# A transformer block on one core: token features spilled in their own layout, one engine's loop written out, one pair of steps on ScalarE swapped

## The chip, the cores and the metric

The kernel runs on one core of a Trainium2 chip. The metric is device time in microseconds (us) of one launch. The engines are named as in the profile: PE is TensorE's matmuls (PEld its weight loads), DVE VectorE, ACT ScalarE, POOL GpSimd, SP SyncE, which here issues all DMAs, in program order, on one queue.

## The reference, cut to what matters

```python
x = x + layernorm(attn(layernorm(x), Wq, Wk, Wv, Wo))          # x: (4, 1024, 512) float32
h = layernorm(x)
gate = h @ spline(gate_cp).T                                   # (4096 tokens, 2048)
up   = h @ spline(up_cp).T
x = x + layernorm((silu(gate) * up) @ spline(down_cp).T)
```

`attn` is attention over the 512 channels (a softmax of 512 x 512 scores for each of the four batches). `spline` fills a dense weight of 2048 x 512 from some 8,000 control points by cubic interpolation, so each run of 128 neighbouring weights is a few cubic pieces.

## The kernel before, in words

An attention block (to about 391 us of the span) and then an FFN block. The FFN never builds the dense gate and up weights. Each token's layernormed row is multiplied by a table of polynomial and window functions, which gives "token features" z: for each of 4 channel tiles (k) 16 unit tiles (t) of 8 powers (f) and 8 window functions. gate and up are then products of z with small coefficient matrices (`s_all`), one pair for each of 16 hidden tiles.

**Groups and steps.** The 4096 tokens are 8 groups (g) of 512, and each group has 16 steps (i), one for each hidden tile; four steps are a quad (j). A step on each engine:

- PE: `gate_up` two steps ahead (gate into `gbank` once `silu_done` says that it was read, up into `ubank` once `inter_done` says so), in every second step `moment_pair`, then `part`, one of 16 pieces of the down projection of the group before (12 matmuls into `ybank`, some pieces three more). In two steps of a quad also `turn` and `products`, which make the features of a tile of tokens six tiles ahead.
- ACT: `high` (cast of inter to f16 `act`, line 1372) of one step and `silu_at` (gated from `gbank`, line 1376) of the step behind it; in between by quad `feats.high` (h_hi), two `z_high` (z_hi, line 1034), `y_out`, `o_norm`, `moment_hi`.
- DVE: `product` (inter, line 1445), and by quad `turn_copy` (hT), `z_low` (z_lo, line 1065), `norm` (xn, line 1049), `low` (h_lo), two statistics, `o_finish` (x_res, line 1476, which adds the residual), in two quads of a group's end also `moment_lo` (line 1451).
- POOL: `low` (act, line 1331) and small scales.

**Turning the features.** The products leave z with (t f) on partitions and (k, tokens) along the row. gate and up want (k f) on partitions and (t, tokens) along the row. So each group is spilled to a DRAM tensor (`token_features`) and loaded again. Before the change the spill does the turn: `spill` (line 1005) issues 12 DMAs of 64 KB for each half of the partitions, each to rows of 1 KB in the order (k, f, t), and `load_z` (lines 1145 and 1147) reads a half in two DMAs, whose rows are 8 KB in one piece. `regroup` in the FFN's SP program does this for the next group after quad 1, when the four tiles are made; PE wants half 0 of it two steps ahead of the group's end (step 14), half 1 eight steps later.

**SP's order around it.** In quad 1 SP does `finish` of tile 0 (the store of x_res, line 1268), then `regroup`, and only then `reload` (the residual of tile 2 into the freed buffer, line 1264), which DVE's `o_finish` wants in step 14. In the other quads `reload` follows `finish` directly, after the store has landed.

**Loops.** All five engines run groups 0, 1, 6 and 7 as straight code and groups 2 to 5 as a loop of two passes (`schedule`), so PE branches back at the end of group 3.

Of the kernel before, what the change touches and what calls it, by code (L numbers as in the profile page):

```python
# [63 lines left out]
def attention_block(nc, x, wq, wk, wvT, wo, x1, raw_ctrl, unit_ctrl, unit_coef, job_in, s_dram, d_dram,  # L64
# [20 lines left out]
    with ExitStack() as ctx:  # L85
# [116 lines left out]
        last_banks = [chain[:, 3, :], chain[:, 2, :]]  # L202
        SPILLS = feats.SPILLS
        assert XR == 4 and NT == 2 * K
# [4 lines left out]
        def _(sp):  # L209
# [40 lines left out]
            def body(b, more):  # L250
# [41 lines left out]
                for t in range(NT):  # L292
                    if not more and t == NT - 1:
                        sp.wait_ge(job_ready, (b + 2) * JOBS)
                        sp.dma_start(d_dram[b], job_out[:]).then_inc(d_stored, 16)
                    sp.wait_ge(x1_ready, b * NT + t + 1)
                    sp.dma_start(x1_t[b * NT + t], x_res[:, t % XR, :]).then_inc(x1_stored[t % XR], 16)
                    if 1 <= t <= NT - XR:
                        load_res(b, t - 1 + XR)
                    elif more and t > NT - XR:  # L300
                        load_res(b + 1, t - 1 + XR - NT)
                    if not more and t < 3:
                        sp.wait_ge(feats.h_normed, t + 1)
                        feats.load(sp, x1_t, XR + t, t)
                    if not more and t < 2:
                        feats.spill(sp, 1, 0, t * SPILLS // 2, (t + 1) * SPILLS // 2)
# [629 lines left out]
class TokenFeatures:  # L936
# [4 lines left out]
    def __init__(self, ctx, nc, K, tiles, spilled):  # L941
# [7 lines left out]
        self.K, self.Q, self.spilled = K, 4, spilled  # L949
        self.SPILLS = 3 * K  # L950
        assert tiles * POWERS == P and tiles * WINDOW == P
# [37 lines left out]

    def spill(self, sp, half, g, first=0, last=None, buf=0):  # L990

        K, tiles = self.K, self.spilled.shape[3] // 2
        high, low = self.z_parts[buf]
        rows = slice(half * P // 2, (half + 1) * P // 2)
        for n in range(first, self.SPILLS if last is None else last):
            if half == 0 and n == 0:
                sp.wait_ge(self.z_hi_done, (g + 1) * self.Q * 2)
            if half == 0 and n == 2 * K:  # L1000
                sp.wait_ge(self.z_ready, (g + 1) * self.Q)
            part, k = (1, 2, 0)[n // K], n % K
            source = (low[rows, k, :], high[rows, k, :], high[rows, K + k, :])[part]
            dest = self.spilled[part, k][:, half * tiles:(half + 1) * tiles, :]
            sp.dma_start(dest.rearrange("f t n -> t f n"), source).then_inc(self.z_spilled[half], 16)

# [88 lines left out]
class FfnInputs:  # L1095
# [43 lines left out]
    def load_z(self, sp, feats, g, par, half):  # L1139

        z = self.z0 if par == 0 else self.z1
        tiles = slice(half * self.half, (half + 1) * self.half)
        sp.wait_ge(feats.z_spilled[half], (g + 1) * feats.SPILLS * 16)
        rows = feats.K * (2 * POWERS + WINDOW)
        sp.dma_start(z[0:rows, tiles, :], feats.spilled[:, :, :, tiles].rearrange("a k f t n -> (a k f) t n")
                     ).then_inc(self.z_loaded[par][half], 16)
        sp.dma_start(z[rows:P, tiles, :], feats.spilled[1, :, :, tiles].rearrange("k f t n -> (k f) t n")
                     ).then_inc(self.z_loaded[par][half], 16)


def ffn_block(nc, x1, feats, ffn_in, d_dram, moments, c_gate, c_up, c_out, out, id16):
# [25 lines left out]
    with ExitStack() as ctx:  # L1177
# [58 lines left out]

        def schedule(engine, quad):
# [8 lines left out]
            with engine.Fori(0, GROUPS // 2 - 2) as pair:  # L1246
                for par in range(2):
                    group(2 * pair + (2 + par), par, pair + 2, Q, Q, True)
            group(GROUPS - 2, 0, GROUPS // 2, 2, 1, False)
            group(GROUPS - 1, 1, GROUPS // 2, 0, 0, False)  # L1250
# [11 lines left out]
        def _(sp):  # L1262
# [15 lines left out]
            def regroup(g, par, loads_before):  # L1278


                for half in range(2):
                    sp.wait_ge(z_loaded[1 - par][half], loads_before * 32)
                feats.spill(sp, 0, g, buf=1 - par)
                feats.spill(sp, 1, g, 0, feats.SPILLS // 2, buf=1 - par)
                ffn_in.load_z(sp, feats, g, par, 0)
                feats.spill(sp, 1, g, feats.SPILLS // 2, buf=1 - par)
                ffn_in.load_z(sp, feats, g, par, 1)

            def quad(g, par, count, j, made, begun, more):
# [77 lines left out]
        def _(act):  # L1367
# [28 lines left out]
            def quad(g, par, count, j, made, begun, more):  # L1396
                for s in range(4):
                    i = 4 * j + s
                    n = g * I + i
                    last = isinstance(n, int) and n >= STEPS - 2  # L1400
                    if not (last and n == STEPS - 1):
                        if i + 1 < I:
                            high(g, n + 1, i + 1, par)
                        else:
                            high(g + 1, n + 1, 0, 1 - par)
                    if not last:
                        silu_at(n + 2, (s + 2) % 4)
                    for before, q in outputs(g, i, 0):
# [12 lines left out]

            silu_at(0, 0)
            feats.high(act, Q + 1)
            high(0, 0, 0, 0)
            silu_at(1, 1)
            feats.z_high(act, Q + 1, 1, 1, z_banks)
# [105 lines left out]
        def _(pe):  # L1532

            def gate_up(n, i, par, count):


                if i % HALF == 0:
                    pe.wait_ge(z_loaded[par][i // HALF], count * 32)
                side, c = i // HALF, i % HALF
# [274 lines left out]
def feature_tables(units, cols_of_x, K, n_ctrl, n_samples):  # L1814
# [58 lines left out]
    assert (high.astype(np.float64) + low == feat).all()  # L1873
    features = np.stack([high, low, pick.astype(np.float16)], 1)
    coef = np.concatenate([coef.reshape(K * POWERS, 5, -1), near.reshape(K * WINDOW, 5, -1)])
    points = np.concatenate([np.repeat(points, n, axis=0) for n in (POWERS, WINDOW)])
    return features, points, coef.astype(np.float32)


def build(nc, x, wq, wk, wvT, wo, raw_ctrl, unit_ctrl, unit_coef, job_in, moments, features, out):  # L1880
# [8 lines left out]
                            kind="Internal").ap()  # L1889
    z_spill = nc.dram_tensor("token_features", (3, hidden // P, POWERS, tiles, 512), F16, kind="Internal").ap()  # L1890
    with ExitStack() as ctx:
# [58 lines left out]
```

## Time and profile before

| | |
|---|---|
| median of 3 runs | 811.36 us (811.29 to 813.33) |
| profiled execution | 814.72 us, span 812.9 us |
| busy share of the span | PE 85%, PEld 59%, DVE 66%, ACT 46%, POOL 54% |
| attention block, FFN block | to about 391 us, from there to 812.9 us |
| first gate matmul of the FFN | 392.1 us |

Times in the trace are from the span's start. A timeline row is start, duration, engine, line, operation, output<-input, shape, count, and in brackets the engine's idle time before it and what ended that. A waits row is the total idle time, the number of waits and the longest one.

### The profile page before, as it was taken

Reading aid. Unit: us, or ns where it says so; the run is one execution under the profiler, and the core shown is the slowest. Engines: PE = TensorE matmul, PEld = TensorE weight load, DVE = VectorE, ACT = ScalarE, POOL = GpSimd, SP = SyncE. Lnnn points to the kernel's source line nnn. Section 1 sums busy time; section 2 is a strip of 40 time slices with the busy share of each in tenths; the row PEclk is TensorE's granted clock in tenths of the full one; section 3 lists DMA queues with packets and bytes.
Section 4 is the critical chain, followed back from the end, with each engine's and each line's share of the span. In section 5 each row is a group of like instructions: output and inputs, shape, how many; then the busy total and the mean of one; then the engine's idle time right before and its main releaser. Section 6 shows DMA issues by size and latency. Waiting matters only on the chain. (4 is left out here: it accounts for less than half of the span.)

```text
span 812.9 us, 16523 instructions
## 1 busy us (share of the span) xinstructions
PE 692.6 (85%) x5872; PEld 482.2 (59%) x5872; DVE 533.7 (66%) x993; ACT 374.3 (46%) x635; POOL 441.7 (54%) x615
## 2 busy tenths in 40 slices
PE   6997899999999999997466987969879698794996
PEld 3765668787778878676123654635546455452555
DVE  7676763696369636746475867959669497672553
ACT  3432233333233323333465755747557476573651
POOL 5199768185928598014254653636536365362542
PEclk9898999999999999999587998989989899897899
DMA  7615556145714474018826153463543635426223
GB/s 242 257 52 180 184 187 216 49 163 178 241 55 148 161 254 132 13 53 228 268 71 169 62 154 112 123 177 113 152 116 113 178 112 137 117 80 164 78 66 104
DMA packets 60687, 115.01 MB, mean 141 GB/s; under 512 B 12880, under 2 KB 25296, under 8 KB 58576
## 3 DMA queue, kind: packets, MB, share of 16 engines
q1 hardware_dynamic: 60624, 114.16, 45.9%
q8 instruction: 41, 0.67, 0.4%
q14 instruction: 22, 0.18, 0.1%
HBM read 81.76 MB, written 32.37 MB: 140 GB/s over the span
## 5 line engine op out<-in xcount | busy, mean ns | idle before, releaser
L1331 POOL TENSOR_TENSOR act<-inter,act 128x512 f16<-128x512 f32 x128 | 158.4, 1245 | 141.2 <-ACT act L1372 141.2
L1445 DVE SCALAR_TENSOR_TENSOR inter<-ubank,c_up,gated 128x512 f32<-128x512 f32 x128 | 95.5, 746 | 62.6 <-ACT gated L1376 61.8
L1586 PE MATMUL ybank<-down,act 128*128 128x160 f16 x512 | 115.4, 243 | 0.0
L1376 ACT ACTIVATE gated<-gbank,c_gate 128x512 f32<-128x512 f32 x128 | 87.7, 685 | 59.9 <-PE gbank L1545 58.2
L1587 PE MATMUL ybank<-down,act 128*128 128x160 f16 x512 | 114.6, 242 | 0.0
L1588 PE MATMUL ybank<-down,act 128*128 128x160 f16 x512 | 114.2, 241 | 0.0
L1372 ACT CAST act<-inter 128x512 f16<-128x512 f32 x128 | 79.2, 619 | 73.1 <-DVE inter L1445 71.6
L1545 PE MATMUL gbank<-z,s_all 128*32 128x512 f16 x512 | 54.7, 418 | 45.4 <-DMA z<-token_features 28.7
L1545 PE MATMUL ubank<-z,s_all 128*32 128x512 f16 x512 | 55.3, 422 | 29.8 <-DVE inter L1445 29.4
L1586 PEld LDWEIGHTS ybank<-down,act 128*128 128x128 f16 x512 | 52.0, 102 | 40.0 <-issue 36.8
L1476 DVE SCALAR_TENSOR_TENSOR x_res<-y,orr,x_res 128x512 f32<-128x512 f32 x32 | 39.2, 1225 | 52.4 <-DMA x_res<-x 44.4
L1545 PEld LDWEIGHTS gbank<-z,s_all 128*32 128x32 f16 x512 | 13.3, 94 | 74.3 <-issue 39.3
L1587 PEld LDWEIGHTS ybank<-down,act 128*128 128x128 f16 x512 | 52.2, 102 | 4.6 <-issue 1.4
L1588 PEld LDWEIGHTS ybank<-down,act 128*128 128x128 f16 x512 | 52.5, 102 | 0.0
L634 DVE SCALAR_TENSOR_TENSOR tu_lo<-chain,tu_hi 128x512 fp32r<-128x512 f32 x32 | 22.1, 690 | 42.2 <-ACT tu_hi L502 42.1
L370 POOL TENSOR_TENSOR yr<-ymv,eps 128x1 f32<-128x1 f32 x32 | 19.9, 622 | 50.3 <-DVE ymv L718 50.2
L502 ACT ACTIVATE tu_hi<-chain 128x512 fp32r<-128x512 f32 x32 | 19.1, 597 | 58.1 <-PE chain L793 58.1
L1561 PE MATMUL mbank<-act,basis 128*32 128x512 f16 x512 | 45.3, 435 | 0.6 <-POOL act L1331 0.6
L791 PE MATMUL chain<-z_hi 128*128 128x512 f16 (+3 forms) x128 | 37.9, 307 | 7.9 <-DVE z_lo L619 7.9
L1049 DVE TENSOR_SCALAR xn<-x_ln,hmv,hr 128x512 f32<-128x512 f32 x32 | 39.1, 1223 | 3.1 <-POOL hr L1018 3.1
L502 ACT ACTIVATE ga_hi<-chain 128x512 fp32r<-128x512 f32 (+3 forms) x32 | 16.5, 517 | 52.0 <-PE chain L793 52.0
L412 POOL TENSOR_TENSOR job<-job 128x640 f32<-128x640 f32 x24 | 38.2, 1593 | 0.8 <-DMA job<-job_in 0.8
(195 smaller groups left out, 1972.0 us busy)
## 6 DMA issues: line engine op xcount, KB each, us to landing
x_ln<-x SPq DMA_DIRECT2D x64, 256.0 KB, 3.3
job<-job_in SPq DMA_DIRECT2D x24, 640.0 KB, 4.6
z<-token_features SPq DMA_DIRECT2D x16, 768.0 KB, 5.7
shared<-x SPq DMA_DIRECT2D x32, 256.0 KB, 2.7
x<-shared SPq DMA_DIRECT2D x32, 256.0 KB, 2.0
token_features<-z_hi SPq DMA_DIRECT2D x128, 64.0 KB
x_res<-x SPq DMA_DIRECT2D x32, 256.0 KB, 2.7
out<-x_res SPq DMA_DIRECT2D x32, 256.0 KB, 2.1
```

The source lines that it names most:

```text
L412: pool.tensor_tensor(job[:, k % 2, 0], job[:, k % 2, 0], job[:, k % 2, 1], ALU.mult).then_inc(job_mult, 1)
L1049: dve.tensor_scalar(self.xn[:, 0, :], self.x_ln[:, slot, :], self.hmv[:, 0:1], self.hr[:, 1:2], ALU.subtract, ALU.mult).then_inc(self.h_no ...
L1331: pool.tensor_tensor(hidden[par][:, i, TOK:2 * TOK], inter[:, i % INTERS, :], hidden[par][:, i, 0:TOK], ALU.subtract).then_inc(inter_ready, 1)
L1372: act.copy(hidden[par][:, i, 0:TOK], inter[:, i % INTERS, :]).then_inc(inter_hi_done, 1)
L1376: act.activation(gated[:, slot % 2, :], gbank[:], ACT.Silu, scale=c_gate[:]).then_inc(silu_done, 1)
L1445: dve.scalar_tensor_tensor(out=inter[:, i % INTERS, :], in0=ubank[:], scalar=c_up[:], in1=gated[:, i % 2, :], op0=ALU.mult, op1=ALU.mult). ...
L1476: dve.scalar_tensor_tensor(out=x_res[:, q % 2, :], in0=y[:, q % 2, :], scalar=orr[:, q, 2:3], in1=x_res[:, q % 2, :], op0=ALU.subtract, op ...
L1545: mm = pe.matmul(bank[rows], s_all[:, side, c, w, rows], z[par][:, i // 4 * 4 + u, :], start=True, stop=True)
L1561: mm = pe.matmul(bank[32 * col:32 * col + 32], basis[:, r, 32 * half:32 * half + 32], hidden[par][:, r, part * TOK:(part + 1) * TOK], star ...
L1586: pe.matmul(out, hidden[par][:, r, high], box[:, 0], start=False, stop=False)
L1587: pe.matmul(out, hidden[par][:, r, high], box[:, 1], start=False, stop=False)
L1588: mm = pe.matmul(out, hidden[par][:, r, low], box[:, 0], start=False, stop=False)
```

## The change

1. `spill` issues three DMAs of 256 KB for a half, each with rows of 4 KB that lie in DRAM as they do in SBUF, and both halves are spilled before the first `load_z`. In the attention block the second half's spill is one piece too, after the first store.
2. `load_z` does the turn: four DMAs of 256 KB for a half, each to 32 partitions, whose source has pieces of 1 KB, 32 KB apart. The rows within a group of 32 partitions are now (f k) and no longer (k f), so the coefficient tables are permuted on the host.
3. SP's `reload` of quad 1 follows its `finish`, ahead of `regroup`.
4. PE's loop over groups 2 to 5 is written out as straight code; the other engines keep it.
5. ACT: `silu_at(n + 2)` comes ahead of `high(n + 1)` in each step, and `silu_at(1)` ahead of `feats.high` and `high` at the block's start.

```diff
     def spill(...):
+        if half == 0:
+            sp.wait_ge(self.z_hi_done, (g + 1) * self.Q * 2)
+        sp.dma_start(self.spilled[1, rows], high[rows, 0:K, :]).then_inc(self.z_spilled[half], 16)
+        sp.dma_start(self.spilled[2, rows], high[rows, K:2 * K, :]).then_inc(self.z_spilled[half], 16)
+        if half == 0:
+            sp.wait_ge(self.z_ready, (g + 1) * self.Q)
+        sp.dma_start(self.spilled[0, rows], low[rows, 0:K, :]).then_inc(self.z_spilled[half], 16)
...
     def load_z(self, sp, feats, g, par, half):
-        rows = feats.K * (2 * POWERS + WINDOW)
-        sp.dma_start(z[0:rows, tiles, :], feats.spilled[:, :, :, tiles].rearrange("a k f t n -> (a k f) t n")
-        sp.dma_start(z[rows:P, tiles, :], feats.spilled[1, :, :, tiles].rearrange("k f t n -> (k f) t n")
+        for at, part in enumerate((0, 1, 2, 1)):
+            source = feats.spilled[part, half * P // 2:(half + 1) * P // 2]
+            sp.dma_start(z[at * group:(at + 1) * group, tiles, :],
+                         source.rearrange("(t f) k n -> (f k) t n", f=POWERS)).then_inc(self.z_loaded[par][half], 16)
...
     def regroup(g, par, loads_before):
                 for half in range(2):
-                    sp.wait_ge(z_loaded[1 - par][half], loads_before * 32)
-                feats.spill(sp, 0, g, buf=1 - par)
-                feats.spill(sp, 1, g, 0, feats.SPILLS // 2, buf=1 - par)
-                ffn_in.load_z(sp, feats, g, par, 0)
-                feats.spill(sp, 1, g, feats.SPILLS // 2, buf=1 - par)
-                ffn_in.load_z(sp, feats, g, par, 1)
+                    sp.wait_ge(z_loaded[1 - par][half], loads_before * 64)
+                    feats.spill(sp, half, g, 1 - par)
+                for half in range(2):
+                    ffn_in.load_z(sp, feats, g, par, half)
...
     def quad(g, par, count, j, made, begun, more):        # SP
                     for before, q in outputs(g, i, 2):
                         finish(before, q)
-                        if j != 1:
-                            reload(before, q)
-                if j == 1:
-                    if not (isinstance(g, int) and g == GROUPS - 1):
-                        regroup(g + 1, 1 - par, count)
-                    for before, q in outputs(g, 6, 2):
                         reload(before, q)
+                if j == 1 and not (isinstance(g, int) and g == GROUPS - 1):
+                    regroup(g + 1, 1 - par, count)
...
     def quad(g, par, count, j, made, begun, more):        # ACT
+                    if not last:
+                        silu_at(n + 2, (s + 2) % 4)
                     if not (last and n == STEPS - 1):
                         if i + 1 < I:
                             high(g, n + 1, i + 1, par)
                         else:
                             high(g + 1, n + 1, 0, 1 - par)
-                    if not last:
-                        silu_at(n + 2, (s + 2) % 4)
...
-            schedule(pe, quad)
+            schedule(pe, quad, loop=False)
```

## Rows read from the trace of the kernel before

**Rows 1.** Timeline of ACT: some silu instructions, each of one step of the FFN.

```profile
404.90 0.68 ACT L1376 ACTIVATE gated<-gbank,c_gate 128x512 f32<-128x512 f32 x1
...
448.17 0.68 ACT L1376 ACTIVATE gated<-gbank,c_gate 128x512 f32<-128x512 f32 x1
...
457.64 0.68 ACT L1376 ACTIVATE gated<-gbank,c_gate 128x512 f32<-128x512 f32 x1
...
467.70 0.68 ACT L1376 ACTIVATE gated<-gbank,c_gate 128x512 f32<-128x512 f32 x1
...
499.26 0.69 ACT L1376 ACTIVATE gated<-gbank,c_gate 128x512 f32<-128x512 f32 x1 [1.55 <-PE gbank L1545]
...
755.28 0.69 ACT L1376 ACTIVATE gated<-gbank,c_gate 128x512 f32<-128x512 f32 x1 [2.44 <-PE gbank L1545]
```

**Rows 2.** Groups by line in the FFN: operation, count, busy us, mean ns.

```profile
L1049 DVE TENSOR_SCALAR xn<-x_ln,hmv,hr 128x512 f32<-128x512 f32 x27 | 35.2, 1304 | 0.9 <-POOL hr L1018 0.9
...
L1451 DVE SCALAR_TENSOR_TENSOR mom_lo<-mbank,mom_hi 128x512 f16<-128x512 f32 x16 | 10.9, 680 | 0.9 <-ACT mom_hi L1382 0.9
```

**Rows 3.** Waits over the whole span: us in total, times, longest us.

```profile
DVE x_res L1476 <- DMA x_res<-x: 44.4, 6, 8.2
...
PE gbank L1545 <- DMA z<-token_features: 28.7, 7, 6.4
...
PE gbank L1545 <- issue: 5.4, 1, 5.4
```

**Rows 4.** Timeline of SP's DMA issues at the end of group 1.

```profile
463.56 0.34 SPq L1268 DMA_DIRECT2D out<-x_res  x1
464.55 4.89 SPq L1005 DMA_DIRECT2D token_features<-z_hi  x8
...
475.61 0.45 SPq L1145 DMA_DIRECT2D z<-token_features  x1
...
484.27 0.31 SPq L1145 DMA_DIRECT2D z<-token_features  x1
...
485.09 0.42 SPq L1264 DMA_DIRECT2D x_res<-x  x1
```

**Rows 5.** Timeline of PE, then of DVE, at the same place.

```profile
482.62 0.40 PE L1545 MATMUL gbank<-z,s_all 128*32 128x512 f16 x4 [3.51 <-DMA z<-token_features]
...
492.72 0.75 DVE L1476 SCALAR_TENSOR_TENSOR x_res<-y,orr,x_res 128x512 f32<-128x512 f32 x1 [8.18 <-DMA x_res<-x]
```

**Rows 6.** Windows there: busy us (instructions) by engine, granted PE clock, DMA share, GB/s.

```profile
470.00:472.00 2.00, 1.58 (x27) 1.38 (x24) 1.96 (x6) 1.13 (x2) 1.69 (x6) 1.00 0.38 105
...
478.00:480.00 2.00, 1.11 (x18) 0.93 (x15) 1.47 (x5) 1.07 (x2) 1.10 (x1) 1.00 0.98 303
...
494.00:496.00 2.00, 1.81 (x14) 0.51 (x15) 2.00 (x4) 1.21 (x2) 1.06 (x1) 0.50 0.57 200
```

**Rows 7.** DMA issues by tensor: count, KB each, median us to landing.

```profile
out<-x_res SPq DMA_DIRECT2D x32, 256.0 KB, 2.1
```

**Rows 8.** Timeline of PE and of ACT in a quad without a stall.

```profile
568.89 0.40 PE L1545 MATMUL gbank<-z,s_all 128*32 128x512 f16 x4
...
565.72 0.60 ACT L1034 ACTIVATE z_hi<-turned 128x512 f16<-128x512 f32 x1
...
569.03 0.62 ACT L1372 CAST act<-inter 128x512 f16<-128x512 f32 x1
569.55 0.68 ACT L1376 ACTIVATE gated<-gbank,c_gate 128x512 f32<-128x512 f32 x1
```

**Rows 9.** Timeline of DVE and of POOL in that quad, and one xn without POOL beside it.

```profile
566.35 0.69 DVE L1065 SCALAR_TENSOR_TENSOR z_lo<-zbank,z_hi 128x512 f16<-128x512 f32 x1 [0.22 <-ACT z_hi L1034]
566.95 1.38 DVE L1049 TENSOR_SCALAR xn<-x_ln,hmv,hr 128x512 f32<-128x512 f32 x1
...
566.90 1.16 POOL L1331 TENSOR_TENSOR act<-inter,act 128x512 f16<-128x512 f32 x1 [0.54 <-ACT act L1372]
...
393.81 0.55 DVE L1049 TENSOR_SCALAR xn<-x_ln,hmv,hr 128x512 f32<-128x512 f32 x1 [0.93 <-POOL hr L1018]
```

More of the change, by code:

```diff
@@ L202, in attention_block @@
         last_banks = [chain[:, 3, :], chain[:, 2, :]]
-        SPILLS = feats.SPILLS
         assert XR == 4 and NT == 2 * K
@@ L304, in body @@
                         feats.load(sp, x1_t, XR + t, t)
-                    if not more and t < 2:
-                        feats.spill(sp, 1, 0, t * SPILLS // 2, (t + 1) * SPILLS // 2)
+                    if not more and t == 0:
+                        feats.spill(sp, 1, 0)
                     if not more and t == 4:
@@ L949, in __init__ @@
         self.K, self.Q, self.spilled = K, 4, spilled
-        self.SPILLS = 3 * K
+        self.SPILLS = 3
         assert tiles * POWERS == P and tiles * WINDOW == P
@@ L988, in load, with spill @@
         sp.dma_start(self.x_ln[:, slot, :], x1_t[m]).then_inc(self.ln_loaded[slot], 16)
-    def spill(self, sp, half, g, first=0, last=None, buf=0):
-        K, tiles = self.K, self.spilled.shape[3] // 2
-        high, low = self.z_parts[buf]
+    def spill(self, sp, half, g, buf=0):
+        K, high, low = self.K, self.z_parts[buf][0], self.z_parts[buf][1]
         rows = slice(half * P // 2, (half + 1) * P // 2)
[L997 to L1005, printed above, removed]
+        if half == 0:
[5 more added lines that the diff above has]
+        sp.dma_start(self.spilled[0, rows], low[rows, 0:K, :]).then_inc(self.z_spilled[half], 16)
     def constants(self, pool):
@@ L1142, in load_z @@
         tiles = slice(half * self.half, (half + 1) * self.half)
+        group = feats.K * POWERS
         sp.wait_ge(feats.z_spilled[half], (g + 1) * feats.SPILLS * 16)
-        rows = feats.K * (2 * POWERS + WINDOW)
-        sp.dma_start(z[0:rows, tiles, :], feats.spilled[:, :, :, tiles].rearrange("a k f t n -> (a k f) t n")
-                     ).then_inc(self.z_loaded[par][half], 16)
-        sp.dma_start(z[rows:P, tiles, :], feats.spilled[1, :, :, tiles].rearrange("k f t n -> (k f) t n")
-                     ).then_inc(self.z_loaded[par][half], 16)
+        for at, part in enumerate((0, 1, 2, 1)):
+            source = feats.spilled[part, half * P // 2:(half + 1) * P // 2]
+            sp.dma_start(z[at * group:(at + 1) * group, tiles, :],
+                         source.rearrange("(t f) k n -> (f k) t n", f=POWERS)).then_inc(self.z_loaded[par][half], 16)
 def ffn_block(nc, x1, feats, ffn_in, d_dram, moments, c_gate, c_up, c_out, out, id16):
@@ L1235, in ffn_block, with schedule @@
         block = ctx.enter_context(nc.Block())
-        def schedule(engine, quad):
+        def schedule(engine, quad, loop=True):
             def group(g, par, count, made, begun, more):
@@ L1245, in schedule @@
             group(1, 1, 1, Q, Q, True)
-            with engine.Fori(0, GROUPS // 2 - 2) as pair:
-                for par in range(2):
-                    group(2 * pair + (2 + par), par, pair + 2, Q, Q, True)
+            if loop:
+                with engine.Fori(0, GROUPS // 2 - 2) as pair:
+                    for par in range(2):
+                        group(2 * pair + (2 + par), par, pair + 2, Q, Q, True)
+            else:
+                for g in range(2, GROUPS - 2):
+                    group(g, g % 2, g // 2 + 1, Q, Q, True)
             group(GROUPS - 2, 0, GROUPS // 2, 2, 1, False)
@@ L1422, in _ @@
             silu_at(0, 0)
+            silu_at(1, 1)
             feats.high(act, Q + 1)
             high(0, 0, 0, 0)
-            silu_at(1, 1)
             feats.z_high(act, Q + 1, 1, 1, z_banks)
@@ L1537, in gate_up @@
                 if i % HALF == 0:
-                    pe.wait_ge(z_loaded[par][i // HALF], count * 32)
+                    pe.wait_ge(z_loaded[par][i // HALF], count * 64)
                 side, c = i // HALF, i % HALF
@@ L1874, in feature_tables @@
     features = np.stack([high, low, pick.astype(np.float16)], 1)
+    coef, near = coef.transpose(1, 0, 2, 3), near.transpose(1, 0, 2, 3)
     coef = np.concatenate([coef.reshape(K * POWERS, 5, -1), near.reshape(K * WINDOW, 5, -1)])
-    points = np.concatenate([np.repeat(points, n, axis=0) for n in (POWERS, WINDOW)])
+    points = np.concatenate([np.tile(points, (n, 1, 1)) for n in (POWERS, WINDOW)])
     return features, points, coef.astype(np.float32)
@@ L1889, in build @@
                             kind="Internal").ap()
-    z_spill = nc.dram_tensor("token_features", (3, hidden // P, POWERS, tiles, 512), F16, kind="Internal").ap()
+    z_spill = nc.dram_tensor("token_features", (3, P, hidden // P, 512), F16, kind="Internal").ap()
     with ExitStack() as ctx:
```

## The prediction

> **What bounds the kernel now.** The FFN block, from 392 us on, is the only part that the change touches in earnest, so I read it by steps. The timeline of ACT comes first, one silu for each step: a quad inside a group takes 467.70 - 457.64 = 10.06 us [rows 1]. From step 3 of group 0 to step 3 of group 7 are seven periods, 755.28 - 404.90 = 350.38 us, 50.05 us each on the mean; the one from group 1 to group 2 is 499.26 - 448.17 = 51.09 us [rows 1]. Four quads would be 40.2 us, and the group's end adds two moment_lo of 0.68 us on DVE [rows 2], so 41.6 us is what a group needs. The reader is to see that some 8 us in each group are a stall, not work.
>
> The waits view names the stall [rows 3]: DVE waits for the residual x_res 44.4 us in 6 waits, and PE for the features z 28.7 us in 7. The SP timeline at one group's end shows why [rows 4]. The spills go out at 4.89 / 8 = 0.61 us each from 464.55 on, 24 of them. The first half's load starts at 475.61, PE wants it at 482.62 - 3.51 = 479.11 and gets it at 482.62 [rows 5]. Then SP stands in front of the second load until 484.27, and the residual for tile 2 goes out only at 485.09, behind 1 MB of z [rows 4]; DVE wants it at 492.72 - 8.18 = 484.54 and has it at 492.72 [rows 5]. After the pause PE's granted clock reads 0.50, that is 1.2 GHz, in 494 to 496 us, against 1.00 in 470 to 472 [rows 6]: the stall is paid a second time by slow matmuls. While the spills run, the DMA engines are only 0.38 busy at 105 GB/s; while z is loaded 0.98 at 303 GB/s [rows 6]. So the spill is bound by SP's issues, not by bytes.
>
> **Part 1, spill and load.** 24 spills of 0.61 us (14.6 us of issue) become 6; 4 loads of z become 8. An issue of 256 KB is 0.34 to 0.42 us (the x_res rows), the dearest issue in sight 0.61 [rows 4]; I take 0.42, since the new spills are as plain as a store of x_res. The move of the reload puts a wait ahead of regroup: the store of tile 0 is issued at 463.56 [rows 4], lands 2.1 us later [rows 7], the reload goes out, and the first spill at about 466.1, 1.5 us later than now. From there it goes by bytes: 1.57 MB of spills at 276 GB/s (105 / 0.38, pieces of 1 KB) to 309 GB/s (303 / 0.98, pieces of 8 KB) [rows 6] is 5.1 to 5.7 us. A store of 256 KB takes 2.1 us [rows 7], of which 0.9 are bytes at these rates, so 1.2 us are overhead. The first half has then landed at about 466.1 + 1.2 + 2.8 = 470.1, the second at 473. The load of half 0 is issued from 470.1 to 471.8, stands behind the second half's spills until about 472.3, and its 1 MB in pieces of 1 KB takes 3.8 us at 276 GB/s; with overhead it lands at about 477.3, 1.8 us ahead of PE's 479.1. Bounds: at half that rate it lands at 481.1, 2 us late and still sooner than now; at 309 GB/s there are 2 us to spare. The z wait goes, by a small margin. Half 1 is wanted eight steps later, some 20 us.
>
> **Part 2, the reload ahead.** The residual of tile 2 is issued at about 465.7 and not at 485.09, 19 us ahead of 484.54. Nothing is left of the 44.4 us [rows 3]. What is queued behind the new waits on SP: the finish of tile 1 and its reload. SP is free of regroup at about 475; the store of tile 1 then stands behind up to 2 MB of z (7.6 us at 276 GB/s) and lands at about 483, the residual of tile 3 at about 486. DVE wants that a quad after tile 2's, at 494.6 or later, so 8 us are to spare.
>
> **Part 3, PE's loop.** PE's branch back costs 5.4 us once, as an "issue" wait [rows 3]. It lies at the end of group 3, today beside an x_res wait, so it is within the seven periods and I don't count it again; without the unrolling it would be what remains there. Group 1 is straight code now, and its quads take the 10.06 us above, so straight code costs nothing that the trace shows.
>
> Sum of parts 1 to 3: 350.38 - 7 x 41.6 = 59.2 us at most. I leave 0.6 us at each group's end, because moment_hi now stands behind one cast more (0.62 us, [rows 8]) and PE's moment rows wait for it: 59.2 - 4.2 = 55.0 us.
>
> **Part 4, silu first.** In a quad two places decide. At its second step PE's gate starts at 568.89 and is done 0.40 later, at 569.29, but ACT casts from 569.03 and starts silu only at 569.55 [rows 8]; with silu first it starts some 0.22 us sooner (after a hop of 0.04), DVE's product follows it, and the chain product, statistics, hT, products, gate starts sooner by as much. At the last step the order costs: the cast now stands between silu and the two z_hi, so the second z_hi (565.72, [rows 8]) ends about 0.5 us later and z_lo, which waits for it already with 0.22 us [rows 9], with it. But xn behind z_lo takes 1.38 us beside a POOL low that starts at 566.90, and 0.55 us where no POOL instruction runs [rows 9]. POOL's low follows the cast, which now ends about 1.1 us later, so xn comes ahead of it: -0.83 + 0.5 = -0.3 us, and the first place, 0.22 us, is what remains as the limit. There are 27 such quads (the count of xn, [rows 2]): 27 x 0.22 = 5.9 us less. Bounds: z_lo late and xn not freed, 27 x 0.5 = 13.5 us more; xn's whole 0.83 us won, 22 us less. I take 5.9, the smallest change that the rows support in both places.
>
> **The turn of the blocks.** In the attention block 18 issues go, so SP comes to the first z load some 1.5 us sooner; I take 1.0 us less for the FFN's start, between 0 and 2.
>
> **Sum:** 55.0 + 5.9 + 1.0 = 61.9 us. The profiled execution took 814.72 us (span 812.9), so one like it would take 752.8; it lay 3.4 us over the median of 811.36, and that median becomes 749.5. I predict 750 us.
>
> The Trainium skill ("DMA: Bandwidth & Descriptors", Rules for kernel authors) speaks against turning in the load: it wants a transpose done by the hardware's own DMA transpose and not by a plain DMA with a rearranged access pattern, and puts 19 times between them. Here the pieces stay 512 elements long, and the spills of before are a rearranged pattern with the same pieces and moved 105 GB/s at a share of 0.38 [rows 6], so the trace does not bear the factor out for them; no row shows it for a load.
>
> **The rivals.**
> - *The z wait stays.* The load in 1 KB pieces, to 32 partitions at a time, is slower than the spills were, or the spill's later start uses up the margin. For it: a margin of only 1.8 us. Against it: the rate of the 1 KB spills. If PE waits as long as now, 28.7 us come back [rows 3]: 750 + 29 = 779; with half of it 764.
> - *Silu first costs.* z_lo comes late and POOL's low meets another of DVE's instructions: 13.5 us more in place of 5.9 less, 769.
> - *More is won.* With xn clear of POOL, DVE has room and the quads fall further, by 22 us and not 5.9: 734. Against it: the gate chain above limits first.
> - *The store of tile 1 comes late.* SP's new order moves the residual wait to tile 3: if z's 2 MB took twice the 7.6 us, it would land near 494 and DVE would wait for part of a clock ramp, some 4 us a group, 778.
> - *Slower than before: the turning load crawls.* Place: PE's wait at step 14. To take back 61.9 us, each of seven ends must stall 8.8 us, so half 0 must land near 488 and not 477.3: its 1 MB taking over 14.5 us, under 72 GB/s. At 20 us for a half the end stalls 14 us: 750 + 7 x 14 = 848. For it: no row shows a load whose source is in strided pieces at that size. Against it: 276 GB/s for such pieces the other way.
>
> (By the Trainium skill's factor of 19 the load would be far beyond that point; it is this rival's support, and the chance below is what the spills' rate leaves of it.)
>
> **How the numbers follow.** Forecast 0.60 (its own range 738 to 764), z wait stays 0.17, silu first costs 0.08, more is won 0.08, tile 1 late 0.03, crawling load 0.04. Range 736 to 779: it takes in all but the last and part of "more is won". A measurement tells 0.3% (2.4 us) from no change; all cases but the last are far faster: faster 0.95, slower 0.04, same 0.01.
>
> **What would show it.** Right: silu periods from group to group of about 42 us; no x_res wait on the residual load in DVE's list; z waits on PE gone or under 1 us each; six spill issues in 3 us; the granted clock at 1.00 across group ends; no "issue" wait of 5 us on PE; quads of 9.8 us; xn near 0.55 us. Wrong: a first z load that lands after PE's step 14 (margin misjudged), quads over 10.1 us (silu first costs), a residual wait at step 2 of a group, or new issue waits on PE in groups 2 to 5.

## The result: 758.0 us, and the profile after

| | before | after | predicted |
|---|---|---|---|
| median, us | 811.33 (810.61 to 813.33) | 758.01 (754.30 to 758.16) | 750 (736 to 779) |
| ratio to before | | 0.9328 [0.9295, 0.9361] | 0.924 |
| profiled execution, us | 814.72 | 758.16 | 752.8 |
| its span, us | 812.9 | 756.4 | |
| seven periods of the FFN, us | 350.38 | 297.62 | 289.5 |

The time lies 8 us above the forecast and inside the forecast's own range. The seven periods are those of the prediction, from step 3 of group 0 to step 3 of group 7, and they hold 52.8 of the 56.6 us by which the two profiled executions differ. ACT's silu shows them, in the timeline of ACT after the change (start, length, line, operation, idle time before it):

```profile
401.14 0.67 ACT L1373 ACTIVATE gated<-gbank,c_gate 128x512 f32<-128x512 f32 x1
...
440.85 0.72 ACT L1373 ACTIVATE gated<-gbank,c_gate 128x512 f32<-128x512 f32 x1
...
450.48 0.69 ACT L1373 ACTIVATE gated<-gbank,c_gate 128x512 f32<-128x512 f32 x1 [0.26 <-PE gbank L1542]
...
460.35 0.69 ACT L1373 ACTIVATE gated<-gbank,c_gate 128x512 f32<-128x512 f32 x1 [0.67 <-PE gbank L1542]
...
481.90 0.69 ACT L1373 ACTIVATE gated<-gbank,c_gate 128x512 f32<-128x512 f32 x1
...
698.76 0.69 ACT L1373 ACTIVATE gated<-gbank,c_gate 128x512 f32<-128x512 f32 x1 [0.87 <-PE gbank L1542]
```

These answer to [rows 1]. The period from group 1 to group 2 is 481.90 - 440.85 = 41.05 us and was 51.09; a quad inside a group takes 460.35 - 450.48 = 9.87 us and took 10.06. The waits of the whole span (us in total, times, longest) answer to [rows 3]:

```profile
PE gbank L1542 <- DMA z<-token_features: 15.9, 7, 3.5
```

DVE's wait for the residual, 44.4 us before, is not in the list any more, nor is PE's wait on its own issue of 5.4 us. PE's wait for z is halved, from 28.7 to 15.9 us, and not gone: this is where the forecast missed. SP's timeline at the end of group 1 shows why (here the length is that of the issue, not of the transfer); it answers to [rows 4]:

```profile
456.43 0.34 SPq L1271 DMA_DIRECT2D out<-x_res  x1
458.51 0.33 SPq L1267 DMA_DIRECT2D x_res<-x  x1
458.94 0.45 SPq L998 DMA_DIRECT2D token_features<-z_hi  x1
459.43 0.60 SPq L999 DMA_DIRECT2D token_features<-z_hi  x1
460.07 0.68 SPq L1002 DMA_DIRECT2D token_features<-z_lo  x1
460.80 1.16 SPq L998 DMA_DIRECT2D token_features<-z_hi  x1
462.01 1.35 SPq L999 DMA_DIRECT2D token_features<-z_hi  x1
463.40 1.05 SPq L1002 DMA_DIRECT2D token_features<-z_lo  x1
464.54 6.26 SPq L1146 DMA_DIRECT2D z<-token_features  x8
...
479.15 0.35 SPq L1267 DMA_DIRECT2D x_res<-x  x1
```

The reader is to see two things. The first three spills take 0.45 to 0.68 us of issue each, the next three 1.05 to 1.35, so the six take 5.5 us where the prediction had 3. And the load, at 464.54, stands 5.6 us behind the first spill, 458.94. PE's timeline shows when z came, at two of the seven ends, and the windows at the same two ends the granted clock (the columns are those of [rows 6]):

```profile
473.95 0.40 PE L1542 MATMUL gbank<-z,s_all 128*32 128x512 f16 x4 [2.20 <-DMA z<-token_features]
...
516.32 0.40 PE L1542 MATMUL gbank<-z,s_all 128*32 128x512 f16 x4 [2.35 <-DMA z<-token_features]
```

```profile
462.00:464.00 2.00, 1.81 (x28) 1.02 (x20) 1.91 (x8) 1.61 (x3) 1.80 (x5) 1.00 0.97 203
...
474.00:476.00 2.00, 2.00 (x33) 1.36 (x34) 0.75 (x1) 1.59 (x3) 0.76 (x2) 1.00 1.16 216
518.00:520.00 2.00, 2.00 (x20) 2.00 (x18) 1.27 (x2) 0.59 (x1) 1.16 (x1) 0.50 1.12 208
```

z came at 473.95 and was wanted 2.20 us sooner, at 471.75. While the halves are spilled (462 to 464) the DMA engines are 0.97 busy and move 203 GB/s; while z is loaded, 1.12 to 1.16 and 208 to 216 GB/s. Before, the same share gave 303 GB/s at 478 to 480 [rows 6], but in another window, while half 1 of z and the residual were loaded, 203 GB/s too:

```profile
488.00:490.00 2.00, 1.56 (x16) 0.72 (x13) 0.00 (x0) 1.63 (x4) 0.00 (x0) 1.00 0.98 203
```

After the wait of 2.20 us the clock stays at 1.00, after that of 2.35 us it reads 0.50, 1.2 GHz, for a stretch.

### The profile page after: what moved, and what is told of

It reads as the page before. It is cut to its first block and busy times, and to the rows that moved or that the text cites. A ratio compares the mean times of both kernels' runs of the same rounds, so it can differ in the third digit from the quotient of the medians.

```text
span 756.4 us, 16316 instructions
## 1 busy us (share of the span) xinstructions
PE 676.6 (89%) x5872; PEld 476.1 (63%) x5872; DVE 512.7 (68%) x993; ACT 365.5 (48%) x635; POOL 430.7 (57%) x615
## 5 line engine op out<-in xcount | busy, mean ns | idle before, releaser
L1328 POOL TENSOR_TENSOR act<-inter,act 128x512 f16<-128x512 f32 x128 | 149.6, 1169 | 135.1 <-ACT act L1369 135.0
L1583 PE MATMUL ybank<-down,act 128*128 128x160 f16 x512 | 112.2, 238 | 0.0
L1584 PE MATMUL ybank<-down,act 128*128 128x160 f16 x512 | 111.5, 237 | 0.0
L1585 PE MATMUL ybank<-down,act 128*128 128x160 f16 x512 | 111.4, 236 | 0.0
L1583 PEld LDWEIGHTS ybank<-down,act 128*128 128x128 f16 x512 | 50.7, 99 | 39.2 <-issue 35.4
L1542 PE MATMUL gbank<-z,s_all 128*32 128x512 f16 x512 | 53.3, 407 | 24.3 <-DMA z<-token_features 15.9
L1542 PE MATMUL ubank<-z,s_all 128*32 128x512 f16 x512 | 52.7, 402 | 8.3 <-DVE inter L1442 7.5
L1584 PEld LDWEIGHTS ybank<-down,act 128*128 128x128 f16 x512 | 51.0, 100 | 3.8
L1585 PEld LDWEIGHTS ybank<-down,act 128*128 128x128 f16 x512 | 51.1, 100 | 0.0
L1473 DVE SCALAR_TENSOR_TENSOR x_res<-y,orr,x_res 128x512 f32<-128x512 f32 x32 | 41.0, 1282 | 13.1 <-ACT y L1391 13.1
L1558 PE MATMUL mbank<-act,basis 128*32 128x512 f16 x512 | 41.4, 402 | 0.6 <-POOL act L1328 0.6
L791 PE MATMUL chain<-z_lo,z_hi 128*128 128x512 f16 (+3 forms) x128 | 38.2, 307 | 0.0
```

What stands on the lines that cost most here:

```text
L791: pe.matmul(out, l_hi, r_lo, start=False, stop=False)
L1328: pool.tensor_tensor(hidden[par][:, i, TOK:2 * TOK], inter[:, i % INTERS, :], hidden[par][:, i, 0:TOK], ALU.subtract).then_inc(inter_ready, 1)
L1473: dve.scalar_tensor_tensor(out=x_res[:, q % 2, :], in0=y[:, q % 2, :], scalar=orr[:, q, 2:3], in1=x_res[:, q % 2, :], op0=ALU.subtract, op ...
L1542: mm = pe.matmul(bank[rows], s_all[:, side, c, w, rows], z[par][:, i // 4 * 4 + u, :], start=True, stop=True)
L1558: mm = pe.matmul(bank[32 * col:32 * col + 32], basis[:, r, 32 * half:32 * half + 32], hidden[par][:, r, part * TOK:(part + 1) * TOK], star ...
L1583: pe.matmul(out, hidden[par][:, r, high], box[:, 0], start=False, stop=False)
```

## The experiments

Every kernel was timed beside the kernel before on the same chip, whose median there was 813 to 814 us; ratios are to that. "Seven periods" are read from each kernel's own profile, as above. They leave out the scatter of the FFN's start: step 3 of group 0, where they begin, lay between 396.8 and 404.9 us in the fourteen profiles, and 4.1 us apart in two kernels that are alike up to there (398.07 and 402.15). They have scatter of their own where PE waits for z: the changed kernel's two profiles give 297.62 and 301.69 us. So a difference of a few us from one profile each is no proof where such waits are left.

**The changed kernel again.** 

> The changed kernel once more, as the base of the runs beside it: 758 us, between 754 and 759.

Measured: 758.53 us (752.91 to 764.18), ratio 0.933 [0.9283, 0.9378]; PE waits for z 17.0 us in 6. This median is the base for the times that follow; periods and waits are compared with the first profile, that of the result.

### Why z still comes late

**The load without its turn.** The load reads each partition's 8 KB as they lie, so it leaves the turn out.

```diff
-                         source.rearrange("(t f) k n -> (f k) t n", f=POWERS)).then_inc(self.z_loaded[par][half], 16)
+                         source.rearrange("(q a) k n -> q (a k) n", a=2)).then_inc(self.z_loaded[par][half], 16)
```

> The changed kernel whose z loads read the same bytes in pieces of 8 KB in a row and leave out the turn (what gate and up then read is not z). My theory: the z wait that is left (15.9 us) comes from the rate of the 1 KB pieces, 205 to 215 GB/s and not 276; at 300 GB/s half 0 lands 1.5 to 1.9 us sooner, the waits fall from 2.3 to about 0.5 us and the granted clock stays at 1.00: 744 us. Rival, the wait comes from SP's order (six spills with 5.5 us of issues, the second half's spills in front of the first load): 757 us, waits of 2 us as before.

Measured: 750.14 us (748.22 to 754.61), ratio 0.924 [0.9199, 0.928]. Its windows at the end of group 1, while z is loaded, and PE's wait there:

```profile
466.00:468.00 2.00, 2.00 (x27) 1.12 (x19) 1.81 (x3) 2.00 (x4) 1.03 (x2) 1.00 0.99 234
468.00:470.00 2.00, 2.00 (x30) 1.40 (x28) 1.49 (x3) 1.42 (x3) 0.60 (x2) 1.00 1.08 246
```

```profile
471.73 0.40 PE L1542 MATMUL gbank<-z,s_all 128*32 128x512 f16 x4 [1.70 <-DMA z<-token_features]
```

The wait remains, 14.4 us in 6. With pieces of 8 KB the load goes at 234 to 246 GB/s and not at 303, so the turn in pieces of 1 KB is a minor part of the low rate. The time came out between the two expectations. Four of the six waits are 1.70 to 1.92 us, where five of seven were 2.09 to 2.35 (the other two are 2.61 and 4.46, and were 1.08 and 3.53), and the clock falls less often behind them. Of the 7.3 us between the two profiled executions only 3.0 lie in the seven periods (294.64), the rest ahead of them.

**Each spill over all 128 partitions.** Three spills of 512 KB in place of six of 256 KB; both halves' loads wait for the three.

```diff
     def spill(self, sp, half, g, buf=0):
...
-        rows = slice(half * P // 2, (half + 1) * P // 2)
+        if half == 1:
+            return
+        rows = slice(0, P)
```

> The changed kernel with each group's six spills of 256 KB (64 partitions each) put together into three of 512 KB over all 128 partitions; both halves' loads wait for the three. Theory A: the spills go at 203 to 213 GB/s because each covers only half of the partitions; over all 128 they go at 300 GB/s or more, the 1.57 MB lands some 2 us sooner, three issues less stand on SP, and PE's z wait of 15.9 us in 7 falls to under 4 us: 745 us. Theory B: the rate has another limit and the first half now waits for all 1.57 MB: the z wait is 15 us or more, 757 us or longer.

Measured: 747.47 us (740.3 to 750.62), ratio 0.9172 [0.9128, 0.9217]. The same window as above, then SP's issues and PE's wait:

```profile
462.00:464.00 2.00, 1.81 (x28) 1.02 (x20) 1.92 (x8) 1.61 (x3) 1.80 (x5) 1.00 1.04 422
```

```profile
458.92 0.38 SPq L1000 DMA_DIRECT2D token_features<-z_hi  x1
...
465.11 4.35 SPq L1147 DMA_DIRECT2D z<-token_features  x8
```

```profile
472.92 0.40 PE L1543 MATMUL gbank<-z,s_all 128*32 128x512 f16 x4 [1.17 <-DMA z<-token_features]
```

The same bytes in the same pieces go at 422 GB/s from 128 partitions and at 203 from 64, at the same share of busy time: theory A on the rate is shown. Each DMA is twice as large as well, but size doesn't explain it: in the changed kernel's trace the 2 KB packets of the store of x_res, 256 KB over 128 partitions, take 0.087 us on the median, 380 GB/s for 16 engines, and the 4 KB packets of the spills 0.32 us, some 206 GB/s, against 0.16 us in this run. The time came out near theory A's, the wait between the two, since the load now waits for all 1.57 MB and goes out at +6.2 us; z comes 1.0 us sooner, not 2, and PE still waits 11.2 us in 7. The seven periods are 8.3 us shorter (289.32): 4.7 us less wait, and two of three drops of the clock avoided, of 1.6 us each (the interval between two silu behind the wait is 4.40 us with the slow clock and 2.81 without; the clock falls at the last end in both kernels).

The load's rate of 208 to 216 GB/s goes with transfers of its own to 32 partitions each; the 303 GB/s of before [rows 6] came from loads of which one in two covers 96. No run here changes the width of the load alone, so for it the cause is supported and not shown. The Trainium skill ("SBUF — State Buffer", Door 1: The DMA port swizzle) has a rule for this: a copy to partitions 0 to 31 or 0 to 63 reaches the same half of the memory's ports for DMA, and only one over all 128 reaches them all. The spills agree with it, 203 against 422 GB/s. It bears on the loads too, which the change narrows to 32 partitions; the prediction weighed another rule.

**Half by half.** SP spills half 0, reloads the residual, loads half 0, and only then spills half 1; half 1 is loaded a quad later.

```diff
                 for half in range(2):
                     sp.wait_ge(z_loaded[1 - par][half], loads_before * 64)
-                    feats.spill(sp, half, g, 1 - par)
-                for half in range(2):
-                    ffn_in.load_z(sp, feats, g, par, half)
+                feats.spill(sp, 0, g, 1 - par)
+                for before, q in between:
+                    reload(before, q)
+                ffn_in.load_z(sp, feats, g, par, 0)
+                feats.spill(sp, 1, g, 1 - par)
...
+                        if j == 2 and more_z:
+                            ffn_in.load_z(sp, feats, g + 1, 1 - par, 1)
```

> The changed kernel with another order on SP: spills of half 0 ahead of the reload (whose wait for the store then runs beside the spills' landing), the load of half 0, only then the spills of half 1, and the load of half 1 after tile 1's store in quad 2. My theory, after the run without the turn: what is left of the z wait is SP's order (half 1's spills and 1.2 us issues in front of the first load), so PE's z waits go, with them the slow clock after them: 7 x 2.3 + 4 x 1.6 = 22 us less, 736 us. Rival, the loads' rate of 205 to 240 GB/s to 32 partitions decides: waits of 1 us or more remain, 750 us; second rival, tile 3's residual stands behind half 1's load and DVE waits at step 2: 750 us or more with residual waits in DVE's list.

Measured: 736.81 us (735.68 to 738.63), ratio 0.9041 [0.9017, 0.9065], the fastest of all. SP's timeline at the same end, then the landing of the load issued at 464.08, the fourth and last of half 0 (it is one of the x4 that start at 462.72), then ACT's silu at the two ends of the seven periods:

```profile
457.25 0.45 SPq L998 DMA_DIRECT2D token_features<-z_hi  x1
457.75 0.60 SPq L999 DMA_DIRECT2D token_features<-z_hi  x1
458.39 0.61 SPq L1002 DMA_DIRECT2D token_features<-z_lo  x1
459.05 1.20 SPq L1267 DMA_DIRECT2D x_res<-x  x1
462.72 1.81 SPq L1146 DMA_DIRECT2D z<-token_features  x4
464.57 0.46 SPq L998 DMA_DIRECT2D token_features<-z_hi  x1
465.08 0.60 SPq L999 DMA_DIRECT2D token_features<-z_hi  x1
465.72 1.04 SPq L1002 DMA_DIRECT2D token_features<-z_lo  x1
```

```profile
L1146 SPq DMA_DIRECT2D z<-token_features x1: 450/450/450, 464.1 to 464.1; - x1
...
DMA to landing us min/median/max: 6.2/6.2/6.2
```

```profile
402.15 0.67 ACT L1381 ACTIVATE gated<-gbank,c_gate 128x512 f32<-128x512 f32 x1
...
678.59 0.69 ACT L1381 ACTIVATE gated<-gbank,c_gate 128x512 f32<-128x512 f32 x1 [0.87 <-PE gbank L1550]
```

Half 0 has landed at 464.08 + 6.2 = 470.3, 13.0 us behind its first spill and not 15.0, and that spill goes out 1.5 us behind the store of tile 0 (at 455.77) and not 2.5, because no reload waits in front of it. PE's wait for z falls to 0.8 us in one, and DVE waits for a residual once, at the last end, so the second rival shows no more than this:

```profile
DVE x_res L1481 <- DMA x_res<-x: 2.0, 1, 2.0
...
PE gbank L1550 <- DMA z<-token_features: 0.8, 1, 0.8
```

The seven periods are 276.44 us. So the order on SP alone, with the narrow transfers and the turn as they were, is worth 297.62 - 276.44 = 21.2 us: 15.1 us of the z wait, 3 x 1.6 = 4.8 us of the slow clock behind it, and 1.3 us besides, net, over all the ends (the clock fell at the first and the last too). By the changed kernel's other profile it is 25.3 us, by the medians 21.7. The edit moves the residual's reload and half 1's spills together; no run parts the two.

### What the other parts are worth

**silu behind again, in both kernels, and alone in the kernel before.** In the changed kernel and in the half-by-half one, ACT's order is put back; in the kernel before, it alone is changed.

```diff
-                    if not last:
-                        silu_at(n + 2, (s + 2) % 4)
...
+                    if not last:
+                        silu_at(n + 2, (s + 2) % 4)
```

> The changed kernel with ACT's old order (silu behind the cast, at the block's start too). My theory: quads inside a group go back from 9.87 to 10.07 us, and xn to 1.38 us beside POOL's low; 27 quads x 0.20 = 5.4 us more, less some 0.3 us at each of seven group ends where the longer quads give z more time: 762 us. Rival, the order is worth nothing and the quads are shorter for another reason (PE's straight code, quieter DMA): 758 us and quads of 9.87.

> The kernel with the halves spilled and loaded in turn (736.8 us), with silu behind the cast and z_hi again, as before the change. Theory A: the 27 quads inside groups go from 9.88 back to 10.07 us (5 us more) and each of 7 group ends loses 0.7 to 1.1 us at its two steps (5 to 8 us): 746 to 750 us. Theory B (the prediction's term): 27 x 0.22 = 5.9 us and nothing at the ends: 742.7 us. Theory C: with the stalls gone the order of ACT's work is no longer what limits: 737 us.

> The kernel before with ACT's new order alone (silu ahead of the cast and the two z_hi), all else as before. Theory A: the quads inside groups fall from 10.07 to 9.88 us and the group ends are stalled by z and the residual as before: 27 x 0.19 = 5 us less, 806 us. Theory B: at the group ends the stall swallows what the quads win ahead of it, since z and the residual land by SP's clock and not by the quads': 811 us.

Measured: from the changed kernel 765.7 us (763.46 to 767.36), ratio 0.9422 [0.9386, 0.9458], 7.2 us more than with the new order and above the 762 of its theory; from the half-by-half kernel 750.25 us (747.99 to 751.48), ratio 0.922 [0.9186, 0.9254], 13.4 us more; alone 812.24 us (809.54 to 815.22), ratio 0.9992 [0.9967, 1.0018], nothing. The seven periods of the second, by silu:

```profile
403.72 0.68 ACT L1381 ACTIVATE gated<-gbank,c_gate 128x512 f32<-128x512 f32 x1
...
689.83 0.69 ACT L1381 ACTIVATE gated<-gbank,c_gate 128x512 f32<-128x512 f32 x1 [0.17 <-PE gbank L1550]
```

286.11 us against 276.44: 9.7 us. A quad inside a group goes from about 9.88 back to 10.07 us, as theory A and the prediction had it, and the first four intervals of groups 2 to 6 from 10.66 to 11.62 us, which the prediction had not. 2.5 of the 9.7 us lie in the first period, which begins at the FFN's start and scatters (39.71 and 42.37 us in the changed kernel's two profiles), so they may not belong to the order. From the changed kernel the quads go back to 10.07 us too, and xn to 1.36 us on the mean, as its theory had it. The waits of the kernel before with the new order alone:

```profile
DVE x_res L1476 <- DMA x_res<-x: 42.7, 6, 7.7
...
PE gbank L1545 <- DMA z<-token_features: 34.3, 7, 6.7
```

Its quads take 9.87 us as well, but what they win is waited for at the group's end: the z wait grows from 28.7 to 34.3 us. Theory B is shown for that kernel.

**TensorE's loop.** It is put back in the changed kernel and in the half-by-half one, and taken away in the kernel before.

```diff
-            schedule(pe, quad, loop=False)
+            schedule(pe, quad)
```

> The changed kernel with PE's loop over groups 2 to 5 put back. My theory: the branch back costs PE some 5.4 us at step 0 of group 4 and nothing lies beside it any more: 763 us, one issue wait of about 5 us on PE's gate. Rival, the branch hides beside the z wait two steps earlier: 758 to 760 us.

> The kernel with the halves spilled and loaded in turn (736.8 us, no z wait left), with TensorE's middle groups in a loop again. No z wait blurs the price of the branch here. Theory A: the branch back costs PE one wait on its own issue of 4 to 5.5 us and, with the clock falling behind it, 5.5 to 6.5 us in all: 743 us. Theory B: the branch hides behind work that PE has no need to hurry with, as it did where a stall stood beside it: 737 us.

> The kernel before with PE's middle groups written out alone. My theory: the branch of 5.4 us lay beside the residual wait of that group's end, so little shows: 809 us, 1 to 3 us less. Rival, it is paid in full: 806 us; second rival, straight code makes new issue waits on PE: over 813 us.

Measured: in the changed kernel 761.13 us (757.44 to 766.72), ratio 0.9372 [0.9327, 0.9418], not to be told from the 758.53 by time; in the half-by-half kernel 743.77 us (738.86 to 744.98), ratio 0.914 [0.9108, 0.9172], 7.0 us more; in the kernel before 815.5 us (810.16 to 819.66), ratio 1.0023 [0.9996, 1.0051], nothing, with no issue wait on PE's gate left. PE at the branch in the half-by-half kernel, then the window behind it:

```profile
557.27 0.40 PE L1550 MATMUL gbank<-z,s_all 128*32 128x512 f16 x4 [4.17 <-issue]
```

```profile
558.00:560.00 2.00, 2.00 (x15) 0.46 (x7) 0.98 (x2) 1.76 (x4) 1.01 (x1) 0.50 0.38 114
```

The branch back costs a wait of 4.17 us and a slow clock behind it: the seven periods are 281.37 us, 4.9 us more. From step 0 of group 4, where the branch lies, to step 0 of group 5 it is 45.39 us against 40.39, so all of it lies there. In the kernel before, where the residual's wait lies beside the branch, it costs nothing. In the changed kernel z's wait lies 9 us ahead of it, and the trace still shows the branch:

```profile
568.10 0.62 PE L1542 MATMUL gbank<-z,s_all 128*32 128x512 f16 x4 [3.93 <-issue]
```

The period with this wait is that run's longest, 48.24 us against 42.66 for the next; the times scatter too much to tell (757.44 to 766.72).

**The residual's reload.** It is put behind regroup again in the changed kernel, and ahead of it alone in the kernel before; the second edit is

```diff
+                        if j != 1:
+                            reload(before, q)
+                if j == 1:
+                    if not (isinstance(g, int) and g == GROUPS - 1):
+                        regroup(g + 1, 1 - par, count)
+                    for before, q in outputs(g, 6, 2):
                         reload(before, q)
-                if j == 1 and not (isinstance(g, int) and g == GROUPS - 1):
-                    regroup(g + 1, 1 - par, count)
```

for the first, and its reverse for the second.

> The changed kernel with SP's reload of quad 1 put back behind regroup. My theory: the few large spills alone end most of the residual wait; the spills start 1.0 to 2.5 us sooner, so the z wait falls from 2.3 to about 1 us, but the residual then stands behind 2 MB of z, lands some 3 us after DVE wants it at six group ends: 758 - 9 + 18 = 767 us. Rival, it was the reload's move that removed the 44 us: about 795 us, residual waits of 7 us again.

> The kernel before with the reload's move alone (old spills, old loads, old order on ACT, PE's loop). My theory: DVE's residual waits are gone (6 ends x some 6 us of silu time), the spills start 1.5 us later and PE waits longer for z at 7 ends (5 us in place of 3.5), the PE branch shows for once with 5 us: 811 - 36 + 10 + 5 = 790 us. Rival, the z wait swallows the gain: 805 us or more.

Measured: behind again 760.84 us (759.95 to 766.47), ratio 0.9357 [0.9318, 0.9397]; ahead alone 801.58 us (795.85 to 805.35), ratio 0.9824 [0.9777, 0.9871]. The waits of the first:

```profile
DVE x_res L1477 <- DMA x_res<-x: 19.5, 6, 3.6
...
PE gbank L1546 <- DMA z<-token_features: 13.8, 7, 3.2
```

And of the second:

```profile
PE gbank L1541 <- DMA z<-token_features: 39.7, 7, 7.4
```

In the kernel before, the move does away with the whole wait for the residual (44.4 us of DVE's idle time), but the time falls by 12.1 us only; PE's wait for z grows by 11.0, to 39.7 us in place of 28.7, and how the rest is lost is not shown. The 801.6 us lie between the two expectations. In the changed kernel the move does away with 19.5 us of DVE's wait and costs PE 2.1 us of z (15.9 against 13.8); by time the two orders can't be told apart, and both expectations were too high. So either edit frees much of the 44.4 us: the move alone all of it, in the kernel before, the shorter spill alone more than half.

## Why the prediction was right, and where it was wrong

The experiments split the seven periods as the prediction did, by way of the half-by-half kernel. Without a z wait and with ACT's old order they are 286.11 us, so the stalls of before were worth 350.38 - 286.11 = 64.3 us; the silu order takes 9.7 more off; the z wait that stayed gives 21.2 back. Each term is from one profile, and another way would part them otherwise: in the changed kernel, with its z wait, the silu order is worth 5.5 us of the periods (303.15 against 297.62).

| term, us | predicted | measured |
|---|---|---|
| stalls gone (parts 1 to 3) | -55.0 | -64.3 |
| silu first (part 4) | -5.9 | -9.7 |
| z wait left, with its clock | 0 | +21.2 |
| sum of the seven periods | -60.9 | -52.8 |
| start of the FFN (turn of the blocks) | -1.0 | -3.8 |

**Part 1 failed in one step: "the z wait goes, by a small margin".** PE wanted z 12.8 us behind the first spill, predicted 13.0; that held. z landed at +15.0 us, predicted +11.2. Of the 3.8 us too little, 1.6 are the first half's spills, whose load goes out at +5.6 and not at +4.0, and 2.2 the load, 473.95 - 464.54 = 9.4 us and not 7.2. Most of both comes from one number: 276 GB/s, worked out as 105 GB/s over a share of 0.38 [rows 6]. A busy share does not scale like that: at a full share the changed kernel's spills and loads went at 203 to 216 GB/s. By an estimate from those rates each half's spills take 1.0 us more than predicted and the load 1.1 more, 3.1 of the 3.8. The sign "six spill issues in 3 us" failed as well (5.5 us), but the issues end at 464.45, when the last spill of the first half is just landing (issued at 460.07, 4.5 us to landing), so they added little. And the prediction saw that half 0's load stands behind half 1's spills, and took that as given, where half by half shows it to be the lever. The wait of some 2 us is that of the prediction's lower bound, though at three quarters of its rate and not half; the rival "the z wait stays", with half of it, had 764 us, and that is the wait that came.

**Part 2 was right on the residual**: no wait of 44.4 us is left, and the move alone is enough for that in the kernel before. It is not the only cause, since behind regroup the changed kernel waits for 19.5 us and not 44.4. Tile 1's store landed late as feared, the reload behind it goes out at 479.15, and DVE did not wait for it; that rival did not come.

**Part 3 was right** that the branch isn't to be counted beside a stall and would remain without one: nothing in the kernel before, 4.9 us where no stall is left.

**The stall term was too small by 9.3 us.** 4.2 of them are the 0.6 us left at each group's end. That was a price of the silu order and belongs to part 4, so like for like the stalls were predicted at 59.2 us and came to 64.3, and the silu order at 1.7 and came to 9.7. The other 5.1 us are there because the prediction took seven equal periods of 41.6 us. Without stalls and with the old order they are 40.52, 40.15, 41.96, 41.90, 41.95, 41.90 and 37.73: the first two and the last are shorter, and the last could have been seen before, where quads fall to 9.26 us from 716.30 on.

**Part 4 was right in its mechanism and short of the group ends.** xn is clear of POOL, as the group by line over the FFN shows, which answers to [rows 2] (mean 537 ns against 1304):

```profile
L1046 DVE TENSOR_SCALAR xn<-x_ln,hmv,hr 128x512 f32<-128x512 f32 x27 | 14.5, 537 | 0.9 <-POOL hr L1015 0.9
```

z_lo waits longer for z_hi, as predicted, in the timeline of DVE, which answers to [rows 9]:

```profile
544.00 0.69 DVE L1062 SCALAR_TENSOR_TENSOR z_lo<-zbank,z_hi 128x512 f16<-128x512 f32 x1 [0.74 <-ACT z_hi L1031]
544.60 0.54 DVE L1046 TENSOR_SCALAR xn<-x_ln,hmv,hr 128x512 f32<-128x512 f32 x1
```

0.74 us against 0.22, so 0.52 later where 0.5 was said, and xn takes 0.54 and not 1.38. The quad gains 0.2 us and not xn's 0.83. That fits the gate chain as the limit, as said: silu now waits for PE's gate inside a quad (0.26 and 0.67 us in the silu rows of the result). No run changes that chain alone. What was missing are the two steps of moment rows at a group's end, some 1 us each time from group 2 to group 6. Predicting 0.6 us of loss there was the wrong sign.

**The turn of the blocks** can't be judged: 3.8 us is within what the FFN's start scatters.

The forecast's error of 8.0 us is thus 21.2 us of stall kept, less 9.3, 3.8 and 2.8 us of terms that were too small, which is 5.3; the rest comes from the profiled execution before, which lay 3.4 us over its median, while that of after lies on it. That the errors largely cancel is luck: the net is better than the parts.

## What to carry to other kernels

Where a transfer is due within a couple of microseconds, order the queue by who is waited for first, one half from end to end before the other half's spill: this was worth 21 us here, where wide spills gained 11 and leaving the turn out 8. Take a transfer's rate from a row at a full share with the same count of partitions; a rate worked out from a low share was a third too high, and that was the forecast's error. An edit that is worth nothing beside a stall can be worth 5 to 13 us when the stall is gone, so judge small edits (order of an engine's work, unrolling) again after the large one.

## What the runs showed of the hardware that was not expected

- A full DMA share says little of the rate: 203 GB/s at a share of 0.97 from 64 partitions, 422 GB/s at 1.04 from 128, for the same bytes in pieces of 4 KB.
- SP's issues lengthen when others stand before them: 0.45 to 0.68 us each for the first three spills, 1.05 to 1.35 for the next three of the same size. Half by half, those next three come behind the load and take 0.46, 0.60 and 1.04, so full DMA engines alone (a share of 0.98 in 464 to 466 there) do not lengthen an issue. What does is not shown.
- The granted clock read 1.00 (2.4 GHz) after a wait of PE of 2.20 us and 0.50 (1.2 GHz) after one of 2.35 us. The fall costs 1.6 us (4.40 against 2.81 us between two silu), on top of the wait. The wait's length alone does not decide: in the changed kernel with silu behind, the clock stayed at 1.00 after a wait of 2.67 us that ended at 610.95 (first row), and with the reload behind it fell after one of 2.01 us that ended at 474.00 (second row). What decides is not shown.

```profile
612.00:614.00 2.00, 2.00 (x36) 1.77 (x36) 1.46 (x2) 1.32 (x3) 0.62 (x2) 1.00 1.09 225
```

```profile
476.00:478.00 2.00, 2.00 (x21) 2.00 (x20) 0.00 (x0) 0.27 (x1) 0.88 (x1) 0.56 1.01 239
```

- PE's branch back is 4.17 us of idle time and 4.9 us in all where PE has work, and nothing that can be measured in the kernel before, beside the residual's wait.
